# A two-layer transformer kernel on one core: down weights queued behind up weights, and a pace for early weight pieces

## The reference, cut to what matters

```python
# layer one
x = x + softmax(...)                        # cross attention, one head
dense_in = rms(layernorm(x), rn_pre1)
dense_out = gelu_tanh(dense_in @ w_gate) * (dense_in @ w_up) @ w_down     # I = 2048
x = x + rms(rms(dense_out, ...) + rms(moe_out, ...), rn_post)             # 8 experts, top 2
# layer two
x = x + attention(...) @ w_out.T            # 16 heads, causal
gate = einsum('bsd,hd->bsh', x, w_gate); up = einsum('bsd,hd->bsh', x, w_up)
x = x + einsum('bsh,dh->bsd', silu(gate) * up, w_down)                    # DIM_HIDDEN = 2048
```

## Time and profile before

| | us |
|---|---|
| median of 3 runs | 1854.75 (1850.45 to 1861.82) |
| the profiled execution | 1854.27 |
| its span, first to last instruction | 1852.5 |
| PE busy | 1693.0 (91%) |
| DVE busy | 1130.6 (61%) |
| ACT busy | 810.7 (44%) |
| mean granted TensorE clock | 0.966 |

### The profile page before, as it was taken

One profiled execution on the slowest core, in us unless ns is written; L12 is line 12 of the kernel. 1 busy time (PEld: TensorE's weight loads), 2 busy tenths in 40 slices (PEclk: granted clock), 3 DMA queues, 4 the chain that ended last, 5 costly groups with the idle time before them and its releaser, 6 DMA issues.

```text
span 1852.5 us, 27428 instructions
## 1 busy us (share of the span) xinstructions
PE 1693.0 (91%) x9460; PEld 1347.2 (73%) x9460; DVE 1130.6 (61%) x2444; ACT 810.7 (44%) x1799; POOL 267.1 (14%) x301
## 2 busy tenths in 40 slices
PE   3688997999989999888999999889999999999998
PEld 2566776878988887676766766677776678678887
DVE  5777679755665646974677764499556663543222
ACT  3566553234665643322565665323155461422111
POOL 1213234610121203220010100132100000000000
PEclk8689998999999999999999999999999999999999
DMA  3324548798888787879889863687862445245562
GB/s 104 114 92 165 182 164 292 245 358 281 262 284 327 248 289 287 308 258 340 298 261 302 283 221 112 233 292 272 301 208 89 120 137 205 80 144 196 195 215 92
DMA packets 135593, 410.06 MB, mean 221 GB/s; under 512 B 16032, under 2 KB 30752, under 8 KB 131744
## 3 DMA queue, kind: packets, MB, share of 16 engines
q1 hardware_dynamic: 123552, 368.98, 58.1%
q0 software_dynamic: 11904, 39.33, 6.5%
HBM read 303.92 MB, written 104.33 MB: 220 GB/s over the span
## 4 chain that ended last, share of the span: by engine, by line
PE 38%; DVE 5%; DMA 4%; ACT 2%; issue 2%; SPq 0%; ACTq 0%; DVEq 0%
PE ps L1226 10%; PE ps L1228 9%; PE ps L1227 9%; PE ps L1380 4%; PE ps L1389 2%; DMA gu<-w_dram 2%; PE ps L1372 2%; DMA raw<-in_ffn_w 1%; ACT Pr L1605 1%; PE ps L1373 1%; DMA w_dram<-raw 0%; DVE mnb L2008 0%; DVE raw L1737 0%; DVE x L2036 0%; PE ps L1232 0%
## 5 line engine op out<-in xcount | busy, mean ns | idle before, releaser
L1226 PE MATMUL ps<-xT,gu 128*128 128x512 f32 (+1 forms) x1392 | 531.2, 382 | 49.6 <-DMA gu<-w_dram 24.7
L1228 PE MATMUL ps<-xT,gu 128*128 128x512 f32 (+1 forms) x1392 | 512.6, 368 | 0.0
L1227 PE MATMUL ps<-xT,gu 128*128 128x512 f32 (+1 forms) x1392 | 512.2, 368 | 0.0
L1226 PEld LDWEIGHTS ps<-xT,gu 128*128 128x128 f32 x1392 | 269.9, 194 | 96.3 <-issue 46.1
L1228 PEld LDWEIGHTS ps<-xT,gu 128*128 128x128 f32 x1392 | 269.2, 193 | 43.1
L1227 PEld LDWEIGHTS ps<-xT,gu 128*128 128x128 f32 x1392 | 269.7, 194 | 35.5
L1226 PE MATMUL ps<-wd,hid 128*128 128x512 f32 x604 | 248.3, 411 | 28.9 <-issue 14.0
L1227 PE MATMUL ps<-wd,hid 128*128 128x512 f32 x604 | 238.0, 394 | 0.0
L1228 PE MATMUL ps<-wd,hid 128*128 128x512 f32 x604 | 237.9, 394 | 0.0
L1437 ACT ACTIVATE hid<-act 128x512 fp32r<-128x512 f32 (+1 forms) x174 | 99.9, 574 | 289.3 <-DVE act L1717 280.8
L1717 DVE TENSOR_TENSOR act<-act,ps 128x512 f32<-128x512 f32 (+1 forms) x174 | 106.7, 613 | 167.7 <-PE ps L1228 158.4
(11 more groups left out here) (283 smaller groups left out, 2362.4 us busy)
## 6 DMA issues: line engine op xcount, KB each, us to landing
gu<-w_dram SPq DMA_DIRECT2D x192, 512.0 KB
raw<-in_ffn_w SPq DMA_DIRECT2D x78, 768.0 KB
wd<-w_dram SPq DMA_DIRECT2D x96, 512.0 KB, 6.2
w_dram<-raw SPq DMA_DIRECT2D x48, 512.0 KB, 4.6
w_dram<-gu SPq DMA_DIRECT2D x16, 1024.0 KB, 10.2
raw<-in_ffn_w POOLq DMA_DIRECT2D x48, 256.0 KB, 5.3
QT<-q_dram SPq DMA_DIRECT2D x48, 256.0 KB, 5.9
y_dram<-x SPq DMA_DIRECT2D x23, 512.0 KB
```

Of the source, the lines that this page charges most:

```text
L1226: mm(out_ap, ah, bh, start=start, stop=False)
L1227: mm(out_ap, ah, bl, start=False, stop=False)
L1228: return mm(out_ap, al, bh, start=False, stop=stop)
```

## The change

Two entries of `held_behind` change. The entry for the first early load becomes a rule for all 48: eload n is held behind the first gate quarter of tile n // 4 of pass (0,3), so four to a tile. A new rule holds the load of the down weights of a tile behind the load of its up weights: `("pre", s, 2)` behind `("pre", s, 1)`. Nothing else is edited. The planner is run again with these two rules, so every order behind the first item that they move can come out differently.

```diff
     def held_behind(item):
 
-        if item == ("eload", 0):
-            return [("gate0", FIRST["F", 0, 3])]
+        if item[0] == "eload":
+            return [("gate0", FIRST["F", 0, 3] + item[1] // 4)]
+        if item[0] == "pre" and item[2] == 2:
+            return [("pre", item[1], 1)]
         if item[0] == "w" and item[1] < 2:
             return [("bet", 0, TB - 1)]
```

## The result

The changed kernel takes 1834.89 us (median; 1831.59 to 1844.24) against 1856.0 us for the kernel before in the same comparison: a ratio of 0.9894 over all four runs of each (the two medians alone would give 0.9886), with a 95% interval from 0.9846 to 0.9942. It is faster, by 1.06%; whether by more than 1% lies inside the interval. The profiled execution has a span of 1831.9 us, 20.6 us less than the one before. Its lines are numbered two higher: the three matmuls are L1228 to L1230, and the gate, up and down loads L970, L973 and L976.

The account below looks back on a forecast made before the run. It took PE's waits for gate and up weights behind down-load bursts as the stake; 6 + 4 + 4.3 + 5.9 + 4.2 (four small waits) = 24.4, less 4 given back, 20.4 us off 1854.27: 1834, range 1820 to 1852.

Parts of the forecast that it names:

- Early loads, nothing: Pass (0,3): pacing the 48 early loads four to a tile gains 0, since the ring of three slots sets the pace.
- 863 us: 6: PE's 7.23 us gate-load wait in pass (0,3): gain 6 us of 9.0 at stake, capped by `QT` loads next in line.
- 1191 and 1204 us: 4: Two gate-load waits in pass (1,0): gain 4 us of 10.9 at stake, because a shorter first wait lengthens the second.
- rival 1: Full DMA stretches: the wait only moves, only isolated waits go; gain about 7 us, time 1847; chance 0.26.
- 1241 and 1318 us: 4.3 + 5.9: Gate-load waits of 2.58 and 3.38 us in layer two: both vanish whole, with 1.7 and 2.5 us of clock.
- Clock, 4.2 in these two and part of the others: Half-level clock around the longer waits: its cost goes with them, 1.7 us at 1241 and 2.5 at 1318.
- Given back, 4: From 1178 to 1285 us: PE waits 4 us more for DVE's adds that free the down banks.
- No cost for late down weights: Downs of each group: the later down loads still land in time where DMA is not full; cost 0.
- Rival 2: Full DMA stretches: down weights come late, PE waits at the first downs; up to 34 us slower, 1888; chance 0.07.
- The queue as the cause of everything: Full DMA stretches, 676 to 1370 us: down-load bursts ahead of gate loads in the queue decide PE's waits; net gain 20.4 us.
- 4 us per place: Each late gate load: having three fewer 512 KB down loads ahead in the queue is worth 4 us.
- rival 3: After about 670 us: the re-planned order adds DVE, ACT and POOL waits; half the gain lost, time 1854; chance 0.10.

Follow-up runs that it names:

- e1: Kernel before with only the pacing rule for early loads, four to a tile; ratio 1.0000 to the kernel before.
- e3: Kernel before with its old orders kept; only in SP's list three of four down loads moved behind the next tile's up load; ratio 0.9965.
- e12: Kernel before with the early-load pacing and the down-load rule for tiles of pass (0,3) alone, planner run again; ratio 1.0027.
- e2: Kernel before with only the rule putting down loads behind up loads, planner run again; ratio 0.9897.
- e4: Changed kernel with its new orders kept; only in SP's list the down loads put back into bursts of four; ratio 1.0119 to the kernel before.
- e8: Changed kernel with the down-load rule limited to tiles of layer two, planner run again; ratio 1.0023 to the kernel before.
- e10: Changed kernel with the middle part's second-pair indirect loads held back to their place in the kernel before, planner run again; ratio 0.9961 to the kernel before.
- e11: Changed kernel with the down-load rule limited to tiles of pass (0,2), planner run again; ratio 0.9955 to the kernel before.
- e7: Changed kernel with the down-load rule limited to layer one, passes (0,2) and (0,3), planner run again; ratio 0.9900 to the kernel before.
- e13: Changed kernel with the planner's look-ahead set from 1.0 to 0.6 us; ratio 0.9928 to the kernel before.

## Why the prediction was right, and where it was not

The time, 1834, is the measured 1834.89, and the main reading held: PE stood for gate weights, and the change takes 20.4 of those 24.7 us away. (That the net sum is 20.4 as well is chance: it had over 4 us of clock in it, and 4 given back.) Most of the signs came too: no four `wd` loads in a row, a gu wait under 8 us, no low clock at tiles h11 of pass (1,0) and h3 of pass (1,1), early loads at their old spacing. But several terms were wrong in ways that cancel.

- *Early loads, nothing.* Right by e1. They go out from 820.0 to 1078.6 us, still 5.5 us apart, held by their ring of slots.
- *863 us: 6.* Near in size: e3 shows 5.6 us at that place, 4.4 of them off the wait, and e12 shows the cap by `QT`. The parts were the other way round. The prediction had 4 to 5 us off the DMA queue and 1.5 off the issue; e3 has 1.3 and 3.1. It had read the earlier trace rows as the burst and then the gate load, but a store and three `KT` loads stand between them on SP. In the changed kernel it is a different story: scores begin ahead of that tile, at 858.5.
- *1191 and 1204 us: 4.* Wrong for the burst alone. With it gone in the old orders the waits are 7.1 us together, against 7.3: the first one went, the second took it over, as rival 1 had it. The way of the second load from issue to use shrank by 2.5 us, not 3.9. Eight loads for `dn` and `xm` stand ahead of it in both kernels. In the changed kernel, where they go out elsewhere, 2.37 us are left.
- *1241 and 1318 us: 4.3 + 5.9.* The idle parts, 2.58 and 3.38, are gone in the changed kernel and in e3, as forecast. But in e3 the time shows little of it: 2.0 us came back as a wait for `QT` at 1349, and the waits for `qb` grew from 2.6 to 6.8.
- *Clock, 4.2 in these two and part of the others.* Failed. By the clock records of the traces the half level (1.2 GHz) covers 37.5 us between 676 and 1370 us both before and after. The stretches went from the waits for weights and came up again at 717, 755, 864, 1267 and 1332 us, each beside a wait of another kind.
- *Given back, 4.* The cause, DVE's work on the down banks, was right, with the place wrong: not between 1178 and 1285 us (DVE is 80% busy from 1158 to 1258), but at 721 us in pass (0,2), 6.0 us. The row that the prediction cited for it, 5.9 us in three waits, was already of pass (0,2): `acc` is the sum of layer one. Over DVE, ACT and POOL the net was -0.8, which is less than such totals move from one execution to the next, and the rows "issue" grew by 4.1.
- *No cost for late down weights.* Right: in no run with the rule does PE wait for `wd`. Rival 2 is out.
- *The queue as the cause of everything.* This step failed in its extent. e3 is close to the prediction's sum made in hardware: the same loads moved past the same gate loads, every other list kept. The sum had 20.4 for it, the chip gave 6.5 (2.4 to 10.6), which is what rival 1 said (7). Queue position was worth less than the 4 us per place, 1.3 to 2.5 where e3 lets it be read, which the prediction had named as what would make it wrong above all; and its sign against the queue as cause, 10 us or more from issue to use without a burst, came too. The rest exists only together with the new orders, which I held for noise with a sign against the kernel (rival 3). I read what a burst costs the tile behind it, and not what it makes the planner do with everything after it.

So the right number rests for the larger part on luck. The wait for weights was read rightly as what stands to be won, and nearly all of it could go; but which part of the edit takes it away was judged wrongly, and had the planner not re-laid its orders, 1834 would have been 15 us too low.

On the rule of the Trainium skill that the prediction weighed ("DMA: Bandwidth & Descriptors", rules for kernel authors: issue early, wait late), the runs side with the trace where the queue is full: e3, which only issues the down loads later, is 0.35% faster, e2, with the new orders too, 1.03%, and e4, which issues them early again, is the slowest of all. But later is not better as such: e8 and e12, which defer them in some passes only, are 0.2 and 0.3% slower.

**Open.** What splits the gain of the new orders between batches 0/1 and 2/3 was not separated further. e10 puts the middle part's place at some 12 us (0.9961 against 0.9894), by way of `QT`, of waits for DVE and of the clock, with whatever else the planner moved for it. e11, with that part as early as e7 has it (1159.6 and 1159.9), gains only 0.45%, so the place alone does not do it; its 12.8 us of gu wait are 8.5 of the 11 us to the changed kernel (0.9955 against 0.9894). Why some orders leave PE longer at the half level than others (e4, e10, e13) is not known. No version was tried that keeps the new orders and moves DVE's middle part off the downs at 721 us, where 6 us lie.

## What to carry to other kernels

When a planner or a static order stands between an edit and the chip, an edit of one rule is two edits: the one written, and the new order of everything behind it. Run them apart (old order with the loads moved, new order with the loads put back) before a gain is put down to either. A planner that has a model of the time can be asked for it: here its end of plan moved by 26 us for the change, where reading single waits gave a wrong split. It is not exact, as e13 shows. And where bulk traffic has to pass through a full queue, the pair e3 and e10 suggests sending it when the next urgent load behind it is for work that follows a long stretch without new weights. When SP's rows are read, look at what stands between two issues, and at whether a long row is one issue or a wait inside a row of several.

## What the hardware showed that I had not expected

- The length of a stall does not say how long the clock stays down. After the wait of 7.23 us in the earlier trace rows the half level lasted 6.8 us; after one of 3.17 us at 862.74 in the changed kernel it lasted 13.7 (864 to 878 us, granted clock 0.51 with PE busy for 12.90 of 14 us), and the same again in e2. Nor does the sum of the waits: from 676 to 1370 us PE stood 55.0 us in the kernel before and 37.9 in the changed one, with 37.5 us of half level in both, while e10 has 58.0 us of it with 47.7 us of waits.
- SP's own issues can stretch in full stretches. In the kernel before, the gate load of tile h8 of pass (1,0) took SP 3.62 us to issue, although its slot had been free since 1186.71; most single loads take 0.32 to 0.45. The DMA share around it is 1.0. What stands behind it in SP's list goes out later by as much.

```profile
1188.30 3.62 SPq L968 DMA_DIRECT2D gu<-w_dram  x1
```
